# Two feed-forward steps moved from the end of a context attention to its first slots

## The reference, cut to what matters

```
x  = layernorm(attn0(x, ctx, bias=2*fside) @ wo + bo + x)     # 16 heads, 64 context tokens
h1 = ln(x); x = quantised_self_attention(h1) + x              # 16 heads, 1024 keys
h2 = ln(x); x = quantised_context_attention(h2, ctx) + x      # 16 heads, 64 context tokens
h3 = ln(x); a, g = split(h3 @ ff_w1 + ff_b1)                  # 512 -> 2 x 2048
x  = (a * gelu(g)) @ ff_w2 + ff_b2 + x                        # 2048 -> 512
```

## Time and profile before

| | us |
|---|---|
| median of three runs | 3263.64 |
| profiled execution, whole | 3268.94 |
| its span | 3267.1 |
| PE busy | 2906.6 (89%) |
| DVE busy | 2171.1 (66%) |
| POOL busy | 1775.2 (54%) |
| ACT busy | 1468.4 (45%) |
| TensorE clock, mean over the span | 0.937 of full |

### The profile page before, as it was taken

The page is one execution under the profiler, slowest core; times in us unless marked ns, Lnnn a source line. Parts: engine busy times, 40 slices in busy tenths (PEclk is TensorE's granted clock), DMA queues, the critical chain, the costliest instruction groups (busy, mean ns, idle before and its releaser), DMA issues.

```text
span 3267.1 us, 50805 instructions
## 1 busy us (share of the span) xinstructions
PE 2906.6 (89%) x19712; PEld 2128.6 (65%) x19712; DVE 2171.1 (66%) x3591; ACT 1468.4 (45%) x2130; POOL 1775.2 (54%) x1698
## 2 busy tenths in 40 slices
PE   6677786898899989899889999899989999899998
PEld 6565554556677656667677656666767756666777
DVE  3467696784665686796675587687574588688521
ACT  5332462673333364474323365375324266275321
POOL 3456484785555185485455186386364277377321
PEclk9888756999999999999999999899999999999999
DMA  8744103335443314324443412333453322232444
GB/s 266 251 180 161 51 16 116 118 122 200 167 167 120 135 40 155 127 98 157 131 178 99 161 53 106 127 111 146 141 186 116 148 78 100 89 143 93 166 168 155
DMA packets 199758, 436.40 MB, mean 134 GB/s; under 512 B 94944, under 2 KB 103392, under 8 KB 182368
## 3 DMA queue, kind: packets, MB, share of 16 engines
q1 hardware_dynamic: 199520, 433.15, 37.1%
HBM read 363.38 MB, written 65.54 MB: 131 GB/s over the span
## 4 chain that ended last, share of the span: by engine, by line
PE 58%; POOL 16%; DVE 11%; issue 6%; ACT 4%; DMA 2%; SPq 1%; POOLq 0%; DVEq 0%; ACTq 0%
PE psum L1756 17%; PE psum L1758 15%; PE psum L1757 15%; POOL w1b L1011 6%; PE psum L2052 4%; PE psum L2040 2%; POOL rec L1006 2%; DVE e L1644 2%; PE psum L2066 1%; POOL u_lo L1030 1%; POOL x L925 1%; POOL fw_lo L1018 1%; ACT e L1315 1%; POOL w_lo L913 1%; DMA fw_lo<-pieces 1%
## 5 line engine op out<-in xcount | busy, mean ns | idle before, releaser
L1315 ACT ACTIVATE e<-e,nb 128x1024 f32<-128x1024 f32 x512 | 588.3, 1149 | 335.0 <-DVE e L1644 331.8
L1644 DVE TENSOR_SCALAR_CACHE_REDUCE e<-psum,nscale 128x1024 f32<-128x1024 f32 x512 | 652.8, 1278 | 76.8 <-POOL w1b L1011 54.4
L1011 POOL TENSOR_SCALAR w1b<-e,rec 128x1024 f16<-128x1024 f32 x512 | 574.6, 1122 | 95.2 <-POOL rec L1006 56.5
L1756 PE MATMUL psum<-h_hi,fw_hi 128*128 128x512 f32 x1024 | 458.1, 447 | 39.8 <-DVE h_lo L1401 14.8
L1657 DVE TENSOR_SCALAR w1T<-psum 128x1024 bf16<-128x1024 f16 x512 | 352.1, 688 | 96.6 <-PE psum L2052 93.1
L2052 PEld LDWEIGHTS psum<-ident,w1b 128*128 128x128 f16 x4096 | 255.8, 104 | 243.9 <-issue 131.5
L2052 PE MATMUL psum<-ident,w1b 128*128 128x128 f16 x4096 | 347.1, 233 | 74.9 <-POOL w1b L1011 46.1
L1757 PE MATMUL psum<-h_lo,fw_hi 128*128 128x512 f32 x1024 | 410.8, 401 | 0.0
L1758 PE MATMUL psum<-h_hi,fw_lo 128*128 128x512 f32 x1024 | 410.7, 401 | 0.0
L919 POOL TENSOR_TENSOR rstd<-ve,mhalf 128x1 f32<-128x1 f32 x128 | 88.5, 691 | 401.4 <-DVE ve L1507 401.4
L1756 PEld LDWEIGHTS psum<-h_hi,fw_hi 128*128 128x128 f32 x1024 | 196.3, 192 | 158.9 <-issue 98.4
(11 more groups left out here) (187 smaller groups left out, 6192.6 us busy)
## 6 DMA issues: line engine op xcount, KB each, us to landing
fw_hi<-pieces SPq DMA_DIRECT2D x168, 512.0 KB, 3.3
fw_lo<-pieces SPq DMA_DIRECT2D x168, 512.0 KB, 4.3
w_hi<-kept SPq DMA_DIRECT2D x45, 1024.0 KB, 4.9
w_lo<-kept SPq DMA_DIRECT2D x45, 1024.0 KB, 7.2
mixed<-mixed SPq DMA_DIRECT2D x32, 1024.0 KB, 5.1
fbias<-in_fside_Bx16xSxS SPq DMA_DIRECT2D x64, 256.0 KB, 3.0
unsplit<-in_L_xattn_ff_w SPq DMA_DIRECT2D x24, 512.0 KB, 5.0
pieces<-fw_hi SPq DMA_DIRECT2D x24, 512.0 KB, 2.7
```

Source lines behind the costliest of these rows:

```text
L1011: pool.tensor_scalar(w1b[u % NH][:], e1[u % NE][:], rec1[:, u % 8:u % 8 + 1], HALF, ALU.mult, ALU.add).then_inc(w1_ready.sem, 1)
L1315: act.activation(e1[s % NE][:], e1[s % NE][:], ACT.Exp, bias=nb1[:, s % NE:s % NE + 1], scale=-1.0, accum_out=sum1[:, s % 8:s % 8 + 1]).th ...
L1644: emptied_bank(dve.tensor_scalar(e1[s % NE][:], psum[:, i:i + 2, :].rearrange("p i n -> p (i n)"), nscale[:, 0:1], LARGEST, ALU.mult, ALU.min,
L1756: pe.matmul(o, s_hi, m_hi, start=first, stop=False)
```

## The change

One line of the plan changes. In a context attention the quarters at the end of each slot were

```
--- before.py
+++ after.py
@@ -75,7 +75,7 @@
     ends = []
     for c in range(NC if in_A else 0):
         for s in range(A_SLOTS):
-            ends.append(4 * in_A * c + (4 if s < A_TAIL else (12, 19, 26, 32)[min(s - A_TAIL, 3)]))
+            ends.append(4 * in_A * c + (min(4 + 2 * s, 12) if s < A_TAIL else (17, 22, 27, 32)[min(s - A_TAIL, 3)]))
     first, start = 4 * NC * in_A, len(ends)
     for s in range(S_SLOTS):
         ends.append(min(first + 4 * in_S, first + 4 * in_S * (s + 1) // (S_SLOTS - 1)))
```

## The result

The changed kernel takes 3282.42 us, the median of four runs (3281.11 to 3286.31), and the kernel before, run on the same chip, 3263.52 (3262.29 to 3265.72): a ratio of 1.005 with a 95% interval of 1.0038 to 1.0063, or 18.9 us more. The forecast was 3281, 17.1 us more than before. The profiled execution took 3286.31 us, of which 3284.5 are span, 17.4 more than the span before.

What follows compares the result with a forecast made beforehand. PE held 58% of the chain, its tail bound partly by the pieces' arrival. Per pair (2.1 + 1.8) + (0.8 + 1.0) = 5.7 us, three pairs 17.1, on 3263.64: 3281 us, own range 3271 to 3291.

Steps and rivals of the forecast that it cites:

- Loop 1.7 us late: First slots of each context attention: moved pairs of quarters only partly fit PE's waits, so PE leaves 1.7 us late.
- The pieces queue behind v1: First-stage tail: piece 2 waits for v1's bytes, usable 9.8 us from v1's issue; PE stands 7.2 us instead of 1.18.
- Rival 2: Tails: pieces do not wait behind v1's bytes, piece 2 usable within 6.6 us of issue; -18 us, 3245 us, chance 0.10.
- norm_T(0) caught behind the wait, 0.4 us: First-stage tail: three norm_T and not two follow the wait for piece 2, adding 0.4 us.
- Clock, 1.8 us in a first stage: Behind the 7 us stall in each first-stage tail: matmuls run at half rate, 3.6 us in place of 1.8.
- Rival 1: Stall without clock cost: clock stays up, or its half-rate stretch replaces one at the tail's end; 3272 us, chance 0.12.
- Rival 3: No change: loop 0.8 us late, clock holds, v1's load runs faster; 3 us, 3267 us, chance 0.08.
- Second stages, +1.8 us: Second-stage tail: 0.8 us for the wait for piece 7 plus 1.0 us for the half-rate clock.
- DVE's moved multiplication: Tail: it waits for the quarter ending step 4, about 963, and is hidden by 5 us before norm_T(2).
- Rival 4: Larger loss: another half-rate stretch follows the stall's in each of six stages, 11 us on top, 3292 us, chance 0.10.

Runs made afterwards that it cites:

- e2: The changed kernel with one step moved and not two, as two pairs of quarters in slots 1 and 2: 3272.46 us, ratio 1.0019.
- e7: The changed kernel with 1 MB left out of v1's load, all but 64 of 2048 columns of its low part: 3269.06 us, ratio 1.0002.
- e3: The changed kernel with SP issuing the pieces of slots 0 to 12 ahead of block v1: 3236.95 us, ratio 0.9922.
- e5: The changed kernel with the tail's first slot ending one quarter earlier, so norm_T(0) stands ahead of the quarter that waits: 3278.49 us, ratio 1.0034.
- e1: The changed kernel with 24 extra matmuls, result unused, ahead of the fifth quarter of each of the six tails: 3270.89 us, ratio 1.0015.
- e8: The changed kernel with pieces ahead of v1, one step moved in first stages and three in second ones: 3254.74 us, ratio 0.9967.

## Why the prediction was right

The forecast was 17.1 us on the profiled execution and came to 17.4 in the span; its steps, in its own order:

- **Loop 1.7 us late.** Measured 1.54 to 1.62 in all six stages. The first two pairs do fill the waits of the earlier trace rows, and POOL's row swallows part of the rest (0.28 us left of 0.45, where 0.11 was worked out: the weights come 0.18 us later and not 0.34). e2 shows where the cost starts: the first two pairs cost 0.12 to 0.45 us in all, so it is mostly the third and the fourth pair that are paid for.
- **The pieces queue behind v1.** PE goes on 9.83 us behind v1's issue (forecast 9.8), 7.14 us of idle (forecast 7.2). e7 shows it from the side of the bytes, e3 from the side of the order. Rival 2, pieces that pass v1, is refuted: piece 2 is usable 8.9 us behind its issue, and the rival needed 6.6. The Trainium skill (DMA: Bandwidth & Descriptors, Queues, rings and completion order) has descriptors consumed in ring order and completion that is not first in, first out for an issuing engine; only the first half shows here: a piece issued 0.9 us behind v1 lands as late as one issued 2.7 us behind it, and the four transfers land in the order of their issue (950.0, 952.5, 953.9 and 955.1).
- **norm_T(0) caught behind the wait, 0.4 us.** e5 gives back 0.3 to 0.8 a stage.
- **Clock, 1.8 us in a first stage.** From 955.20 to 969.25 PE needs 14.05 us for what takes 12.4 at full rate, 1.65, and e1 gives 1.6 and 2.1 for the two stages that compare. Without the fall of the clock, in e1, these two end 2.0 us later than before, where the forecast had 2.1. Rival 1 is refuted in both its forms: the clock does fall at the stall, and the stretch at the tail's end is not replaced by it but comes as well, in six places where it was in five. 3272 was reached only by e1, which keeps PE busy. Rival 3 goes with them: it needed the clock up and a loop 0.8 us late. The Trainium skill (TensorE: Matmul & The Clock Gate, Part 1) puts the ramp penalty under 1% of a typical kernel span and warns against fitting a specific count of slow matmuls. Its figure agrees (11.4 us by e1 are 0.35%). But a figure under 1% is no reason to leave the term out here: this change as a whole is worth 0.5%, and without the term the forecast would have been 8.7 us, half of what was measured.
- **Second stages, +1.8 us.** This is the one term that was off: 2.23, 2.21 and 2.28. The half-rate stretch behind the wait was taken over from the earlier trace rows as 3.6 us long; it lasted 4.7 (1076.97 to 1081.7), worth 2.3 us. Piece 7, for which the forecast kept 0.8 us of wait, is covered by it. In e1, with the clock up, piece 7 is waited for by 0.34 to 0.43 us and the second stages end 0.7 us later than before: so the 0.8 was near, and the clock's share was 1.5 us where the forecast had 1.0. Taken together 0.4 too little in each of three stages.
- **DVE's moved multiplication.** Hidden, as said: last z 3.5 us ahead of the transposes.

- **Rival 4, further half-rate stretches.** It did not come behind the stalls, but in one place behind a tail: 1.5 us in the first pair, where the kernel before has none.

What came right by offset: the tails make 18.7 us where the steps sum to 17.1, the stretches behind them add 2.0 that no step had, and 3.2 us come back elsewhere in that one execution. By the medians it is 18.9 for 17.1.

## What to carry to other kernels

An engine's wait at the end of a stage may belong to a queue and not to its own work: then taking work out of that stage turns into wait, one for one, until the load that is late is issued sooner or has fewer bytes ahead of it. Ask of each load what stands ahead of it on its queue and which buffer's release it waits for, and change order and plan together: here each alone lost (+18.9 and +9.7 us) and the two together gained 29 by the medians, of which about 22 can be placed. Five of the six stalls of PE cost 1.5 to 2.1 us at half rate on top of their length by e1 (the sixth does not compare), so two short waits (e3's of 1.2 us, with the clock up) were cheaper than one of 2.4 (e8's).

## What the runs showed of the hardware

- The granted clock falls while PE waits and comes back late: full until 951.9, 3.8 us into the idle, then at 1.2 GHz until 3.5 us after work resumed, and until 4.7 us after it in the second stage with the same wait, where it fell 5.0 us into the idle. Behind shorter waits it fell later than the wait's end: about 0.5 us after PE had work again in e3 (wait 2.75), 1.4 us after it in e8 (wait 2.40).
- The same idle of 2.20 us ahead of q1 is followed by 3 to 4 us at 1.2 GHz in five of six places before, in all six of the changed kernel and of e5, in one of six in e1, and in none in e3. Each such stretch is worth 1.1 to 1.6 us, and a half of what e1 gained, a third of what e3 gained on the kernel before's pairs, lies there. What decides it these runs do not show.
- Transfers of one queue arrive one behind the other at 401 to 442 GB/s with the DMA share at 1: 3.1 MB in the 9.8 us from v1's issue, and 2.0 to 2.5 us less with 1 MB less. In the first tail of the changed kernel the four transfers, issued from 945.37 to 946.68, land at 950.0, 952.5, 953.9 and 955.1.
